# Post-norm decoder block: the expert biases written into PSUM by ScalarE in place of bias-row products on TensorE, and one buffer for both transposed inputs

## The reference

```
x  = layernorm(x + mamba(x))                 # state-space scan, 512 inner channels, 16 states
x  = layernorm(x + cross_attention(x, ctx))  # 16 heads of 16, 154 context rows
x  = layernorm(x + moe(x))                   # 4 experts, the 2 best of each token
# one expert e of moe:
h  = relu(ln(x @ W1[e] + b1[e]) * g1[e] + be1[e])
y  = ln(h @ W2[e] + b2[e]) * g2[e] + be2[e]
moe(x) = sum over e of weight[token, e] * y
```

## Time and profile before

| | |
|---|---|
| median of 3 runs | 1922.05 us (1920.25 to 1922.87) |
| the profiled execution, its own time | 1920.12 us |
| its span, first to last instruction | 1918.3 us |
| mean granted TensorE clock | 0.883 of full speed |
| PE, DVE busy | 1525.0 us (79%), 1524.0 us (79%) |
| ACT, POOL busy | 1012.7 us (53%), 899.5 us (47%) |
| first part (mamba) | up to about 1057 us |
| turns 0 to 3 begin with their scores at | 1125, 1316, 1512 and 1714 us |

### The profile page before, as it was taken

How to read it: one execution, slowest core, us unless ns; L and a number is a source line. 1 busy time by engine, 2 the same in 40 slices (tenths; PEclk the granted TensorE clock), 3 DMA queues, 4 the chain that set the end, 5 groups by cost and what they waited for, 6 DMA issues and landing times. The chain is left out here.

```text
span 1918.3 us, 26696 instructions
## 1 busy us (share of the span) xinstructions
PE 1525.0 (79%) x8112; PEld 1080.4 (56%) x8112; DVE 1524.0 (79%) x2861; ACT 1012.7 (53%) x2226; POOL 899.5 (47%) x717
## 2 busy tenths in 40 slices
PE   4777778877887778877756689988998899899890
PEld 3666667756676656666645435564555545564470
DVE  1899999999999999999996443696449734874578
ACT  3667876677667876687752234125512461246240
POOL 0677767777777777877674000004400440035004
PEclk9888889888988889888966779989989998899895
DMA  4301110111011110111100301000010000000000
GB/s 137 123 30 50 62 57 5 62 63 62 26 36 62 62 62 1 62 62 56 47 20 6 117 1 45 4 1 1 23 48 1 2 23 23 1 1 1 23 1 22
DMA packets 38437, 71.24 MB, mean 37 GB/s; under 512 B 3697, under 2 KB 31954, under 8 KB 33970
## 3 DMA queue, kind: packets, MB, share of 16 engines
q1 hardware_dynamic: 38290, 69.45, 10.6%
HBM read 60.79 MB, written 8.65 MB: 36 GB/s over the span
## 5 line engine op out<-in xcount | busy, mean ns | idle before, releaser
L605 POOL TENSOR_TENSOR state_c<-state,c_bc 128x1024 f32<-128x1024 f32 x256 | 603.3, 2360 | 232.8 <-DVE state L668 220.1
L668 DVE TENSOR_TENSOR_SCAN state<-decay,carry,bu_ps 128x256 f32<-128x256 f32 x768 | 527.5, 727 | 0.0
L485 ACT ACTIVATE decay<-dt_sb,negA 128x256 f32<-128x256 f32 x1024 | 433.7, 498 | 3.1 <-issue 3.1
L1261 POOL TENSOR_TENSOR big<-big,g_sb 128x1024 f32<-128x1024 f32 x29 | 68.9, 2376 | 667.2 <-DVE big L1366 610.6
L653 DVE TENSOR_TENSOR bu_ps<-u_sb,b_ps 128x512 f32<-128x512 f32 x512 | 344.5, 673 | 43.4 <-POOL u_sb L546 36.4
L350 PE MATMUL y_ps<-ident_sb,state_c 128*128 128x128 f32 x2048 | 305.4, 299 | 20.1 <-DVE yg L636 12.6
L350 PEld LDWEIGHTS y_ps<-ident_sb,state_c 128*128 128x128 f32 x2048 | 264.4, 156 | 51.6 <-POOL state_c L605 24.8
L271 PE MATMUL w_ps<-xT_sb,w_conv 128*128 128x256 f32 (+1 forms) x1024 | 235.8, 383 | 13.3 <-DVE w_conv L706 11.9
L271 PEld LDWEIGHTS w_ps<-xT_sb,w_conv 128*128 128x128 f32 x1024 | 191.6, 192 | 39.5 <-DVE w_conv L706 11.9
L668 DVE TENSOR_TENSOR_SCAN state<-decay,bu_ps 128x256 f32<-128x256 f32 x256 | 160.1, 665 | 0.0
L334 PE MATMUL b_ps<-parts,sel_bc_sb 96*128 96x256 bf16 x256 | 76.8, 301 | 103.5 <-DVE bu_ps L653 95.7
(11 more groups left out here) (166 smaller groups left out, 2406.4 us busy)
## 6 DMA issues: line engine op xcount, KB each, us to landing
c_bc<-c_scratch SPq DMA_DIRECT2D x32, 1024.0 KB, 5.8
res<-in_x SPq DMA_DIRECT2D x16, 256.0 KB, 2.8
x_scratch<-res SPq DMA_DIRECT2D x16, 256.0 KB, 7.2
stage<-x_scratch SPq DMA_DIRECT2D x4, 1024.0 KB, 7.6
xa<-x_scratch SPq DMA_DIRECT2D x4, 1024.0 KB, 5.4
out_x<-acc SPq DMA_DIRECT2D x4, 1024.0 KB, 4.5
xT_sb<-in_xT SPq DMA_DIRECT2D x12, 259.0 KB, 3.0
w_sb<-in_w SPq DMA_DIRECT2D x2, 1024.0 KB, 13.1
```

Of the source, the lines that this page charges most:

```text
L485: nc.scalar.activation(decay[:, n % RING, j, :], dt_sb[:, i[1] % 2, j, :], ACT.Exp, scale=negA[:, j * NS + n:j * NS + n + 1]).then_inc(s_d ...
L605: nc.gpsimd.tensor_tensor(state_c[:, n % RING, :, :], state[:, n % RING, :, :], c_bc[:, q, n, :].unsqueeze(1).to_broadcast([P, CT, TC]), A ...
L668: nc.vector.tensor_tensor_scan(state[:, n % RING, j, :], decay[:, n % RING, j, :], bu_ps[m % 3][:, e * TC:(e + 1) * TC], carry[:, n, j:j + ...
```

## The change

ACT writes the biases into the two banks of a tile before PE's products reach them (`preset`), and those products then all add to what the bank holds (`start=False`). The bias values lie on all 128 partitions in a new fp32 tile `biases`, filled by one broadcast transfer. Gone are the 128 bias products, `brow`, `ones3_sb`, and DVE's splitting of the rows in the setup. PE's waits for the copies (`s_l1c`, `s_l2c`) become waits for the preset (`s_pre`). `xT` becomes another name for `x1T`, which frees the space that `biases` takes. In `transposes` only the first of the four that share a bank carries the start flag.

```diff
-        brow = sb("brow", [3 * BLK, 2 * E * DM], BF16)
+        biases = sb("biases", [P, 2, E * DM])
...
-        xT = sb("xT2_sb", [P, KT, L])
+        xT = x1T
...
-            sp.dma_start(big[0:3 * BLK, 1, 0:2, :], bias_rows.rearrange("q (a n) -> q a n", a=2)).then_inc(s_brow, 16)
             load_x1(0, xa[:, :, :], s_x)
             sp.dma_start(g2_sb[:, :], g2.partition_broadcast(P)).then_inc(s_const, 16)
             sp.dma_start(be2_sb[:, :], be2.partition_broadcast(P)).then_inc(s_const, 16)
+            sp.dma_start(biases[:, :, :].rearrange("p a n -> p (a n)"), bias_rows.partition_broadcast(P)).then_inc(s_const, 16)
...
-                        last = nc.tensor.transpose(ps[:, bank + u, i * P:(i + 1) * P],
-                                                   src[:, half * TG + i, k * P:(k + 1) * P], ident_sb[:, :])
+                        last = nc.tensor.matmul(ps[:, bank + u, i * P:(i + 1) * P],
+                                                src[:, half * TG + i, k * P:(k + 1) * P], ident_sb[:, :],
+                                                start=i == 0, stop=True, is_transpose=True, skip_group_check=True)
...
-                    if t >= 2:
-                        pe.wait_ge(s_l1c, b * TT + t - 1)
+                    pe.wait_ge(s_pre, b * 2 * TT + t + 1)
                     for h in range(2):
                         dst = ps[:, 2 * (t % 2) + h, :]
-                        nc.tensor.matmul(dst, ones3_sb[:, :], brow[:, h * HALF:(h + 1) * HALF], start=True, stop=False)
...
-                        if t >= 2:
-                            pe.wait_ge(s_l2c, b * TT + t - 1)
-                        else:
-                            pe.wait_ge(s_l1c, b * TT + TT)
+                        pe.wait_ge(s_pre, b * 2 * TT + (TT + t + 1))
...
-                            if e % 2 == 0:
-                                nc.tensor.matmul(ps[:, 2 * (t % 2) + e // 2, :], ones3_sb[:, :],
-                                                 brow[:, E * DM + e * DM:E * DM + (e + 2) * DM],
-                                                 start=True, stop=False, skip_group_check=True)
...
+                def preset(t):
+
+                    if t < 2:
+                        act.wait_ge(s_ytc, b * TRB + TRB)
+                    elif t < TT + 2:
+                        act.wait_ge(s_l1c, b * TT + t - 1)
+                    else:
+                        act.wait_ge(s_l2c, b * TT + t - TT - 1)
+                    nc.scalar.activation(ps[:, 2 * (t % 2):2 * (t % 2) + 2, :],
+                                         biases[:, t // TT, :].rearrange("p (a n) -> p a n", a=2),
+                                         ACT.Copy).then_inc(s_pre, 1)
...
                 copy_transposed(b, xT, 0, s_yt, s_ytc)
+                preset(0)
+                preset(1)
                 for t in range(TT):
                     act.wait_ge(s_l1, b * TT + t + 1)
                     nc.scalar.activation(big[:, t // TG, t % TG, :].rearrange("p (a n) -> p a n", a=2),
                                          ps[:, 2 * (t % 2):2 * (t % 2) + 2, :], ACT.Copy).then_inc(s_l1c, 1)
+                    preset(t + 2)
...
                         nc.scalar.activation(big[:, n, i, :].rearrange("p (a n) -> p a n", a=2),
                                              ps[:, 2 * (t % 2):2 * (t % 2) + 2, :], ACT.Copy).then_inc(s_l2c, 1)
+                        if t + 2 < TT:
+                            preset(TT + t + 2)
                         if t == TG + 1:
                             guess(b, 3)
...
-            nc.vector.tensor_copy(brow[:, :], row).then_inc(s_split, 1)
-            dve.wait_ge(s_split, 1)
-            nc.vector.tensor_tensor(left, row, brow[:, :], ALU.subtract).then_inc(s_split, 1)
```

More of the change, by code:

```diff
@@ L741, in attn_ffn_block @@
         bqk_sb, bv_sb, swap_sb, gw_sb, gb_sb = (w[n] for n in ("bqk", "bv", "swap", "gw", "gb"))
-        lnp_sb, ones3_sb = (w[n] for n in ("lnp", "ones3"))
+        lnp_sb = w["lnp"]
         g2_sb = sb("g2_sb", [P, E * DM])
@@ L1558, in _ @@
             keys_values(0, 0)
-            dve.wait_ge(s_brow, 16)
-            row = big[0:3 * BLK, 1, 0:2, :].rearrange("p a n -> p (a n)")
-            left = big[0:3 * BLK, 1, 2:4, :].rearrange("p a n -> p (a n)")
-            nc.vector.tensor_copy(brow[:, :], row).then_inc(s_split, 1)
-            dve.wait_ge(s_split, 1)
-            nc.vector.tensor_tensor(left, row, brow[:, :], ALU.subtract).then_inc(s_split, 1)
-            dve.wait_ge(s_split, 2)
-            for q in (1, 2):
-                nc.vector.tensor_copy(brow[BLK * q:BLK * q + BLK, :], left[BLK * q:BLK * q + BLK, :]).then_inc(s_split, 1)
-            dve.wait_ge(s_split, 4)
-            nc.vector.tensor_tensor(left[2 * BLK:3 * BLK, :], left[2 * BLK:3 * BLK, :], brow[2 * BLK:3 * BLK, :],
-                                    ALU.subtract).then_inc(s_split, 1)
-            dve.wait_ge(s_split, 5)
-            nc.vector.tensor_copy(brow[2 * BLK:3 * BLK, :], left[2 * BLK:3 * BLK, :]).then_inc(s_split, 1)
-            dve.wait_ge(s_split, 6)
             maxima(0)
@@ L1581, in decoder_block @@
 def decoder_block(nc, x, xT, w_in, cw, w_x, w_out, par, ident, sel_bc, sel_p, ctxT, wq, wk, wv, wo, bqk, bv, swap,
-                  w1, w2, gw, gb, lnp, bias_rows, ones3, g2, be2, before, out):
+                  w1, w2, gw, gb, lnp, bias_rows, g2, be2, before, out):
     c_dram = nc.dram_tensor("c_scratch", (NCH * NS, TC), F32).ap()
@@ L1595, in decoder_block @@
                 ("gb", [P, E], gb.partition_broadcast(P)),
[L1596 to L1598 removed]
+                ("lnp", [P, 2 * E * KT], lnp)):
+            w[name] = ctx.enter_context(nc.sbuf_tensor(name + "_sb", shape, F32))
             ahead.append((w[name][tuple(slice(None) for _ in shape)], source))
@@ L1617, in _constants @@
             swap[BLK * j + HD + i, BLK * j + HD + i] = 1
-    ones3 = np.zeros((3 * BLK, P), np.uint16)
-    ones3[0::BLK] = one
     before = np.tri(E, k=-1, dtype=np.float32).reshape(E * E)
-    return dict(ident=np.eye(P, dtype=np.float32), sel_bc=sel_bc, sel_p=sel_p, swap=swap, ones3=ones3, before=before)
+    return dict(ident=np.eye(P, dtype=np.float32), sel_bc=sel_bc, sel_p=sel_p, swap=swap, before=before)
 def _layout(inputs):
@@ L1664 @@
 _ARGS = ["x", "xT", "w_in", "cw", "w_x", "w_out", "par", "ident", "sel_bc", "sel_p", "ctxT", "wq", "wk", "wv", "wo",
-         "bqk", "bv", "swap", "w1", "w2", "gw", "gb", "lnp", "bias_rows", "ones3", "g2", "be2", "before"]
+         "bqk", "bv", "swap", "w1", "w2", "gw", "gb", "lnp", "bias_rows", "g2", "be2", "before"]
 def kernel(**inputs):
```

14 lines of the change are left out of this document (4 added, 10 removed).

## The result

| | before | changed |
|---|---|---|
| median | 1922.28 us (6 runs, 1920.25 to 1926.72) | 1915.11 us (6 runs, 1913.75 to 1917.39) |
| ratio to before, 95% interval | | 0.996 (0.9949 to 0.9971) |
| the profiled execution, its own time | 1920.12 us | 1915.81 us |
| its span | 1918.3 us | 1914.0 us |
| mean granted TensorE clock | 0.883 | 0.883 |

The change makes the kernel 7 us faster, 0.3 to 0.5%. The page of the changed kernel, against the earlier trace rows: PE lost 23.4 us of busy time, ACT gained 65.0, and DVE's share of the last chain grew from 10% to 13%.

A forecast was written before the change was run, and what follows sets the result against it. PE and DVE are equally busy, the last chain mostly over PE. Gains of 4.2 + 2.7 + 4 x 0.0 = 6.9 us off 1920.1 give 1913.2, plus 1.9 for the median: 1915.1 us; range 1906.5 to 1920.5.

The forecast's parts named there:

- Preset, 1.02 us: ACT's bias write to PSUM lasts as long as a tile's copy, 1.02 us; in ACT's way it costs 1.07.
- Second layer, 0.0 a turn: Each turn, opening to guess: 1.5 gained, 1.07 lost at handover, 0.65 gained, 1.07 lost before the guess; sum 0.0 us.
- First layer, turn 3, 2.7: DVE's measurement of tile 7 comes 2.7 us earlier: 1.5 up to the guess, plus 1.2 of DVE's idle time.
- First layer, turns 0 to 2, 1.4 each: DVE's idle time before early maxima shrinks by 0.89 plus 0.5, so 1.4 us a turn, 4.2 in three.
- Its term for a product behind the rounds, 0.22: Removing a bias product behind the rounds saves 0.22 us: 0.32 on the chain, less 0.10 for its weight load.
- about 0.5 of the 0.56 goes: Turns 0 to 2, first layer: DVE's 0.56 us idle before a maximum depends on two bias products; about 0.5 goes.
- Nothing for the setup and the sharing: Dropping DVE's splitting of bias rows, the biases' transfer and the shared xT buffer change the time by nothing.
- A: Rival: PE's clock also falls at turn 1's last transposes and second-layer opening, costing 4.4 us; 1919.5 us, chance 0.14.
- D: Rival: the clock falls in fewer places; turns 0 and 2 lose slow stretches, 4.4 us each; 1906.3 us, chance 0.10.
- B: Rival: the clock falls at the second layer's handover in all turns, 3 us each; 1927 us, chance 0.06.
- C: Rival: the preset is dearer, nine times in ACT's way; at 1.35 us 1918.1, at 1.8 no gain; chance 0.06.
- E: Rival: DVE takes all the gain of turns 0 to 2, leaving turn 3's 2.7 us; 1919.4 us, chance 0.08.

The follow-up runs named there:

- experiment 3: Kernel before with shared buffer and presets in the second layer alone, bias products kept in the first: 1920.49 us, ratio 0.9982.
- 11: Kernel before with shared buffer, plus products of zeros filling PE's waits at the end of the rounds of turns 0 to 2: 1913.17 us.
- 12: Changed kernel plus products of zeros filling PE's waits at the end of the rounds of turns 0 to 2: 1911.0 us.
- Experiment 1: Kernel before with one edit, the two transposed inputs sharing a buffer: 1920.9 us against 1922.0, ratio 0.9993.
- 4: Changed kernel with three presets of each turn (tiles 5 and 7 of the second layer, 6 of the first) moved out of ACT's way: 1905.73 us.
- 6: Changed kernel with only the second layer's last preset moved, from before the guess to behind it: 1910.86 us.
- experiment 7: Changed kernel with each preset issued twice, the second behind a wait for the first: 1931.11 us, ratio 1.0043.
- 10: Changed kernel with three presets per turn moved, plus products of zeros filling PE's waits at the end of the rounds of turns 0 to 2: 1899.82 us.
- experiment 5: Changed kernel with neither presets nor bias products, biases left out of both layers, waits for the copies as before: 1904.21 us, ratio 0.9914.
- experiment 9: Changed kernel with 64 bf16 products of zeros where the first layer's bias products stood: 1921.74 us, ratio 0.9992.
- 2: Kernel before with shared buffer and presets in the first layer alone, bias products kept in the second: 1914.84 us, ratio 0.9957.

## Why the prediction was right, and where it was not

The time, 1915.1, is what was measured, and part of that is luck: the change itself gave some 5 us where the sum had 6.9, and TensorE's clock, which the sum left as it was, made up the rest. Point by point:

- **Preset, 1.02 us.** Measured 1.03; in ACT's way 1.10 from copy to relu or guess instead of 1.07. Writing PSUM is no quicker here than reading it (1.024 us). The sentence of the Trainium skill, "ScalarE: Activation LUTs", section "Step-by-step: what each stage is for", is about PSUM against SBUF as the destination; the two instructions differ in their source as well, so this pair does not test it, but the 0.8 us that the prediction allowed for it did not come.
- **Second layer, 0.0 a turn.** -0.44 and +0.5 at equal clock (experiment 3), where the sum had -0.43 and +0.42. Right, with the two waits foreseen: 1.56 at the handover, 7.48, 7.17 and 7.07 early in turns 1 to 3.
- **First layer, turn 3, 2.7.** 2.4. The step holds: copies are 3.44 apart instead of 3.87, the guess is delayed by 1.10, DVE's idle 1.19 is gone. The ten bias products ahead of the copy of tile 4 gave 2.1 us from the gate on (26.50 to 24.39), not 2.6.
- **First layer, turns 0 to 2, 1.4 each.** This step failed twice. Its term for a product behind the rounds, 0.22, was mis-sized: half tiles with a round between them start 2.65 us apart in place of 2.78 (L958 at 1221.17 and 1223.82, before at 1213.90 and 1216.68), so 0.13: the chain has 0.74 for the round, 0.32 for the bias product and 1.72 for the fp32 products before, and 0.74 and 1.91 after, so the fp32 product now in front takes back 0.19, where the sum allowed 0.10 for its weight load. With it "about 0.5 of the 0.56 goes" was wrong: 0.13 went, 0.43 stayed. Without clock effects the three turns gained 1.0 to 1.2 (experiments 11 and 12). And the clock's price was added in two of the three turns: 1.7 at turn 1's transposes, 0.9 or 3.0 between turn 0's gate and its first maximum, though in the profile with 3.0 the gate itself began 1.0 us earlier.
- **Nothing for the setup and the sharing.** Experiment 1 for the sharing; DVE's split was not tried by itself; in the profiles whose first gate ran near full clock the way there from 1070 us is 137.2 us with it and without.
- **The clock, left at what it was.** Rivals A and D stood as alternatives to the forecast; parts of both came true at once. A came at the transposes of turn 1 in all eight profiles whose first layer has other than bias products there (none, or zeros) and which have no fillers, and in none of the three with them; its second leg, the opening, did not come in the changed kernel (it did in experiments 4 and 6, 0.50 in the first 6 us). D came as the openings: 4.1 us over the four turns, where the sum had none. The prediction named a different clock in the openings as what would make it wrong, and by that measure its account was: at equal clock the change takes off some 5 us (5.7 in the first layers less 0.1 to 0.2 in each second one), the other 2 are the clock's balance, a term that the sum had put at nothing. That the total met the forecast is luck to that extent.
- **B, C and E.** B did not come behind the change's waits of 1.56; in experiment 7, behind 2.62, it came in three of four turns. What the Trainium skill, "TensorE: Matmul & The Clock Gate", section "HAM oscillation — how this bites in real kernels", tells of is waits for transfers longer than either, so it spoke for the rivals less than the prediction had it. C is excluded by the presets' durations. E is excluded too: turn 2 gained.
- **Slips in the sums.** Turn 3's PE gain, 2 x 0.45 + 14 x 0.22, is 4.0 and not 3.9; the preset's bounds give 1914.3 to 1918.1 and not 1912 to 1918; and the range, which was to take in D, ends 0.2 above D's 1906.3. None of them touches the forecast.

How the clock's gains came about stays open. That PE's idleness at the end of the rounds lets it fall is shown by experiments 10 to 12: with the fillers the last transposes took 1.97 us in all nine turns, without them 3.2 to 3.7 in 30 of 33. Why turn 1's transposes fell in the changed kernel and not before is open: the wait ahead is 1.83 us in both; with neither presets nor products (experiment 5) they took 3.67, and with presets and products of zeros (experiment 9) 3.24. And the gain of about 2 us by the clock is read from a profile of each kernel; that it is as large in the medians is not shown. The openings of turns 0 and 3 are fast in the changed kernel's first profile and in those of experiments 2, 6 and 7, but turn 0's is slow in the changed kernel's second.

## What to carry to other kernels

Work that is moved to a half-idle engine costs nothing where it lies in that engine's idle time, and its full length where it stands between two others that wait in turn; list what follows it in that engine's order, and issue it one step later if it isn't due yet. Here the place of twelve of 64 presets, nine of them in the way of something by the prediction's count, decided over more than half of what there was to gain (1922 to 1915.1 with them, 1905.7 with them moved, 1904.2 with no bias at all). Where TensorE waits again and again for a microsecond or two, read the granted clock of the stretch behind each wait before adding up durations, and look at more than one profile: an edit of 0.2 us per product can be outweighed by 1.7 us of clock.

## What the runs showed of the hardware that was not expected

- The clock's falls are tied to the code but not fixed by it. The kernel before and experiment 1 repeat them within 0.1 us, the changed kernel's two profiles differ in three places (gate 6.15 and 4.04; opening of turn 0 0.93 and 0.58, of turn 2 0.60 and 0.93). The Trainium skill, "TensorE: Matmul & The Clock Gate", section "What's actually happening", says that the count of slow products varies between runs of one kernel; this pair of profiles agrees.
- Products of zeros can keep the clock up: 23 of them a turn, 0.22 us each, in waits that lay idle, took 5.9 us off (1905.7 to 1899.8, on two chips whose runs of before agree within 0.3).
- A copy on ACT takes as long towards PSUM (1.028 us) as from it (1.024).
- The same first part differs by up to 5.8 us between executions.
